# Fused gated transformer block on one core: another order of the first loads, statistics before tables, and the skip terms made by ScalarE and added a quad of heads at a time

## The reference

```python
x = x + jnp.tanh(g_xattn[0]) * _L0_xattn_ref(ctx_2048, ctx_2048, _layernorm(x, axis=-1), ssm_kernel, D, 8)
# _L0_xattn_ref: 16 heads of 8 channels, k = v = context, q = layernorm(x)
kv = jnp.einsum('bhil,bhjl->bijhl', k_, v_)            # pair products inside a head
y = irfft(rfft(kv, n=2L) * rfft(ssm_kernel, n=2L))[..., :L]   # causal convolution along l
out = y + kv * D[None, None, None, :, None]            # skip term, one number per head
out = jnp.einsum('bijhl,bhil->bjhl', out, q_)
```

## Time and profile before

| what | before |
|---|---|
| median of 3 runs | 958.02 us (956.0 to 959.27) |
| the profiled execution's own time | 956.07 us |
| its span in the trace | 953.6 us |
| PE busy | 910.1 us (95%) |
| DVE, ACT, POOL busy | 605.7, 545.4, 200.7 us |
| first block | 0 to 115.7 us of the span |

### The profile page before, as it was taken

The page is one execution under the profiler, slowest core; times in us unless marked ns, Lnnn a source line. Parts: engine busy times, 40 slices in busy tenths (PEclk is TensorE's granted clock), DMA queues, the critical chain, the costliest instruction groups (busy, mean ns, idle before and its releaser), DMA issues.

```text
span 953.6 us, 13986 instructions
## 1 busy us (share of the span) xinstructions
PE 910.1 (95%) x4744; PEld 723.5 (76%) x4744; DVE 605.7 (64%) x1396; ACT 545.4 (57%) x947; POOL 200.7 (21%) x171
## 2 busy tenths in 40 slices
PE   5799889999999999979999988999999999999998
PEld 5799758877788888846666666778788888888886
DVE  6678654555564565478888765656955466556554
ACT  3222043433444335458889675777777777777775
POOL 5899400000000001137777530000000000000000
PEclk9899999999999999999999998999999999999999
DMA  8100120323211351024554305444444344444443
GB/s 299 62 1 1 34 84 17 107 80 114 94 51 35 96 187 58 32 88 156 176 169 156 121 7 166 133 133 132 133 146 150 98 133 133 147 149 136 139 129 109
DMA packets 58101, 104.62 MB, mean 110 GB/s; under 512 B 7312, under 2 KB 13840, under 8 KB 57648
## 3 DMA queue, kind: packets, MB, share of 16 engines
q1 hardware_dynamic: 57312, 103.60, 34.0%
q10 hardware_dynamic: 720, 0.14, 0.1%
HBM read 101.29 MB, written 2.42 MB: 109 GB/s over the span
## 4 chain that ended last, share of the span: by engine, by line
PE 49%; DVE 3%; ACT 2%; issue 1%; DMA 1%; POOL 0%; DVEq 0%; SPq 0%; ACTq 0%; POOLq 0%
PE bank L1111 19%; PE bank L1078 18%; PE bank L1370 3%; PE bank L1381 2%; PE bank L1363 1%; PE bank L1362 1%; PE bank L1358 1%; PE bank L1390 1%; PE bank L534 1%; PE bank L770 1%; DVE X L668 0%; DMA Gf<-gates 0%; DVE shifted_scores L1560 0%; PE bank L752 0%; DVE max L1554 0%
## 5 line engine op out<-in xcount | busy, mean ns | idle before, releaser
L1078 PE MATMUL bank<-xhf,whif 128*128 128x512 f32 x528 | 212.0, 401 | 1.5 <-ACT rf L848 1.5
L1078 PE MATMUL bank<-xlf,whif 128*128 128x512 f32 x528 | 208.2, 394 | 0.0
L1078 PE MATMUL bank<-xhf,wlof 128*128 128x512 f32 x528 | 208.1, 394 | 0.0
L867 ACT ACTIVATE yhif<-yf 128x512 fp32r<-128x512 f32 x200 | 124.1, 622 | 86.6 <-DVE yf L952 82.5
L966 DVE TENSOR_TENSOR yf<-yf,Gf 128x512 f32<-128x512 f32 x125 | 86.5, 692 | 129.3 <-ACT yf L856 122.1
L1111 PE MATMUL bank<-yhif,whif 128*128 128x512 f32 x400 | 159.5, 399 | 7.0 <-DVE ylof L731 6.5
L1111 PE MATMUL bank<-yhif,wlof 128*128 128x512 f32 x400 | 157.9, 395 | 0.0
L1111 PE MATMUL bank<-ylof,whif 128*128 128x512 f32 x400 | 156.9, 392 | 0.0
L731 DVE TENSOR_TENSOR ylof<-yf,yhif 128x512 fp32r<-128x512 f32 x196 | 134.4, 687 | 30.0 <-ACT yhif L867 29.7
L850 ACT ACTIVATE rf<-bank 128x512 f32<-128x512 f32 x136 | 81.0, 596 | 80.7 <-PE bank L1078 80.6
L1078 PEld LDWEIGHTS bank<-xhf,whif 128*128 128x128 f32 x528 | 99.3, 188 | 24.5 <-ACT rf L848 1.9
(11 more groups left out here) (135 smaller groups left out, 1212.2 us busy)
## 6 DMA issues: line engine op xcount, KB each, us to landing
Gf<-gates SPq DMA_DIRECT2D x157, 256.0 KB, 3.7
wrawf<-in_wu SPq DMA_DIRECT2D x68, 256.0 KB, 2.6
k_blocks_sb<-in_k_blk SPq DMA_DIRECT2D x64, 256.0 KB, 4.1
wrawf<-in_wu SPq DMA_DIRECT2D x32, 384.0 KB, 3.2
v_slot<-in_v_rows SPq DMA_DIRECT2D x16, 256.0 KB, 2.7
ctx_windows<-in_ctx_win SPq DMA_DIRECT2D x3, 1024.0 KB, 11.7
toeplitz<-in_kpad SPq DMA_DIRECT2D x4, 512.0 KB, 9.2
X<-in_x SPq DMA_DIRECT2D x4, 512.0 KB, 9.3
```

Source lines behind the costliest of these rows:

```text
L867: act.activation(yhi[:, K % S, :], y[:, K % S, :], ACT.Copy).then_inc(s_yh, 1)
L1078: last = pe.matmul(o, w_[:, Nu % S, wc], x_[:, c, xs], start=(m == 0), stop=(m == 5))
```

## The change

The first load of input rows now goes ahead of the first windows and the first table. ACT issues its constants in the order D, anti-diagonal, identity instead of identity, anti-diagonal, D. ACT makes the skip blocks D[h] * anti in a new tile `skip` (16 activations of 128x128), and DVE adds them to the table with one TENSOR_TENSOR of 128x4x128 for each quad instead of four SCALAR_TENSOR_TENSOR. On DVE the statistics of part 0 stand ahead of the tables, and the tables of quads 2 and 3 stand between weighings. POOL does part 0 ahead of `pairs(1)`. PE turns group 0 after step 1 instead of step 2. The wait for the tanh gate moves from the start of group 0 to group 1.

```diff
@@ sync
+                    rows(0)
                     window_quad(0)
                     kernel_table(0)
-                    rows(0)
@@ gpsimd
                     pairs(0)
-                    pairs(1)
                     pool.wait_ge(s_mh, 1)
                     deviations(pool, "a", 0)
                     shifts(pool, "a", 0)
+                    pairs(1)
                     pairs(2)
                     pairs(3)
@@ scalar
+                    act.dma_start(dbc[:], d_skip.partition_broadcast(P)).then_inc(s_ca, 16)
+                    act.dma_start(anti[:], anti_c).then_inc(s_ca, 16)
                     act.dma_start(ident[:], ident_c).then_inc(s_c, 16)
-                    act.dma_start(anti[:], anti_c).then_inc(s_ca, 16)
-                    act.dma_start(dbc[:], d_skip.partition_broadcast(P)).then_inc(s_ca, 16)
...
+                    def skip_blocks(hq):
+                        for h in range(4 * hq, 4 * hq + 4):
+                            last = act.activation(skip[:, h, :], anti[:], ACT.Copy, scale=dbc[:, h:h + 1])
+                        last.then_inc(s_sk, 1)
+
+                    act.wait_ge(s_ca, 32)
+                    skip_blocks(0)
                     squares(0)
+                    for hq in range(1, 4):
+                        skip_blocks(hq)
+                    normed(0)
+                    squares(1)
                     act.wait_ge(s_tl, 32)
                     act.activation(tg[:], graw[:], ACT.Tanh).then_inc(s_tg, 1)
-                    squares(1)
-                    normed(0)
@@ tensor
                             convolve(g, r // 2, r % 2)
-                            if g == 0 and r == 2:
+                            if g == 0 and r == 1:
                                 for half in range(2):
                                     turn(0, half)
@@ vector
                         dve.wait_ge(s_kt[hq], 16)
-                        for h in range(4 * hq, 4 * hq + 4):
-                            last = dve.scalar_tensor_tensor(TM[:, h, 0:P], anti[:], dbc[:, h:h + 1], TM[:, h, 0:P], ALU.mult, ALU.add)
-                        last.then_inc(s_td, 1)
+                        dve.wait_ge(s_sk, hq + 1)
+                        hs = slice(4 * hq, 4 * hq + 4)
+                        dve.tensor_tensor(TM[:, hs, 0:P], TM[:, hs, 0:P], skip[:, hs, :], ALU.add).then_inc(s_td, 1)
...
-                    dve.wait_ge(s_ca, 32)
-                    table(0)
                     input_moments(0)
                     dve.wait_ge(s_st, st.n)
                     variances(dve, "a", 0)
                     negated(dve, "a", 0)
-                    for hq in range(1, 4):
+                    for hq in range(2):
                         table(hq)
-                    dve.wait_ge(s_tg, 1)
                     for g in range(NG):
                         for r in range(8):
                             weigh(g, r // 2, r % 2)
+                            if g == 0 and r in (0, 2):
+                                table(2 + r // 2)
                             if g == 0 and r < 3:
                                 input_moments(r + 1)
...
+                            if g == 1 and r == 0:
+                                dve.wait_ge(s_tg, 1)
```

More of the change, by code:

```diff
@@ L165, in build @@
             dbc = sb("dbc", [P, NH0], ctx=pa)
+            skip = sb("skip_blocks", [P, NH0, P], ctx=pa)
             s_r = deviation_sems["a"][2]
@@ L173, in build @@
             s_td = sem("a_table_ready")
+            s_sk = sem("a_skip_blocks_ready")
             s_kv = sem("a_pairs_ready")
```

## The result

The changed kernel takes 961.48 us (median of 20 runs, 955.24 to 964.96), the kernel before 958.06 in the same comparison (20 runs): a ratio of 1.0039, 95% interval 1.0025 to 1.0052. It is slower by 3.4 us, outside the range. Measured again later (e12), it was 961.53 against 958.23, ratio 1.0037 (1.0024 to 1.0049). Two executions of e7, at 1147 and 2296 us, were in a slower state and are left out of its median and ratio.

The account below looks back on a forecast made before the run. The prediction took group 1's turn, behind DVE's and POOL's nearly level chains, as the bound. A start 2 to 3.5 us earlier would shrink to 0.15 to 0.2 in the block: -0.2 from 958.02, 957.8 us, range 955.3 to 960.3.

Parts of the forecast that it names:

- What bounds it: Group 1's turn on PE at 37.16 us, behind DVE's chain ending at 32.27 and POOL's at 31.35.
- the floor of 31.35: End of POOL's large product of pairs(5), the earliest start of its power of part 1, then at 32.35.
- the landing of the identity: Identity load third on ACT's queue: lands between 4.8 and 7.4 us, where it landed first at 3.88.
- The slower rival: Late identity delays PE's warming-up and the first weighing; slower by 2.9 us from a landing at 9.8; chance 0.10.
- w: Start of DVE's first weighing: 17.4 us, up to 18.9 by the identity or 20.0 by ACT, against 20.93.
- 1.2 us of waiting on POOL: Waiting counted in DVE's chain when setting w = 18.4, beyond which each us of w costs one at the turn.
- the 12.72: DVE's chain from the first weighing to vpe's end without waits on POOL: 11.34 us plus 1.38 for two tables.
- The sum: The whole forecast change, -0.2 us; in it a table addition holds POOL up for 0.69.
- term for step 6: PE's step behind the wait takes 2.91 us at 1.2 GHz, a loss of 1.34 expected to stay the same.
- ceiling: Most the power of part 1 could gain with DVE early: 1.00 us, from 32.35 to 31.35.
- The second rival: Clearly faster: floor 1.0, clock 1.34 and group 1's load 0.6 us earlier, 954.9 or less; chance 0.11.
- The wait for POOL: Some DVE operations wait for a whole POOL multiplication under way, such as a TENSOR_SCALAR of 1.62 us.

Follow-up runs that it names:

- e12: The changed kernel measured again with no edit: 961.53 us against 958.23 for the kernel before, ratio 1.0037.
- e7: The kernel before with ACT's constants in the order D, anti-diagonal, identity and nothing else: 960.19 us against 957.88, ratio 1.0029.
- e10: e6 with POOL's power of part 1 ahead of the products of quad 5, fills of 18 and 10 matmuls: 954.94 us, ratio 0.9965.
- e6: The changed kernel with the identity first and unused matmuls, 24 ahead of the turn, 10 ahead of the last reductions: 955.38 us, ratio 0.9976.
- e11: The kernel before with only ACT's skip blocks and one TENSOR_TENSOR a quad, all orders as before: 956.94 us, ratio 0.9984.
- e3: The kernel before with 14 unused matmuls filling PE's idle time ahead of the turn: 955.57 us, ratio 0.9975.
- e8: The kernel before with unused matmuls, 14 ahead of the turn and 10 ahead of the last reductions: 954.54 us, ratio 0.9964.
- e5: The changed kernel with the identity issued first again on ACT's queue: 956.86 us against 957.88 for the kernel before, ratio 0.9993.
- e9: The changed kernel, identity third, with PE warming up on a tile DVE sets, 24 matmuls, no load needed: 957.96 us against 958.23, ratio 1.000.
- e4: The changed kernel with unused matmuls, 20 ahead of the turn and 10 ahead of the last reductions: 956.81 us, ratio 0.9984.
- e2: The changed kernel with 20 unused matmuls filling PE's idle time ahead of the turn: 958.68 us, ratio 1.0004.
- the first profile: The first profiled execution of the changed kernel, with no further edit: 958.30 us.

## Why the prediction was wrong

- *What bounds it: right.* The turn of group 1 is the point through which the first 37 us act, and two chains stand in front of it. e10 moved POOL's half and the turn came 1.43 us earlier than in e6; e11 moved DVE's half and the power started at 31.31, at the floor of 31.35.
- *The failed step: the landing of the identity,* "between 4.8 and 7.4". Its upper end came from one row, D landing third at 7.36. In the five profiles with the new loads and the identity third it landed once at 6.96 and four times at 9.2 to 9.6; third beside the old loads at 7.92. The row of before was no bound either: D in its old third place landed at 8.6 to 8.7 in the profiles of e3 and e8.
- *The slower rival was the mechanism,* with the chance of 0.10 that the bound gave it. Its threshold was a landing at 9.8 and a first weighing at 21.3 for 2.9 us. Measured in e12: 9.62, 21.37 and a turn 2.14 us late, where the rival's 1 us for each beyond w = 18.4 gives 3.0; it counted 1.2 us of waiting on POOL in DVE's chain, which took 13.04 in e12, 0.3 over the 12.72. e5 shows it by taking it away (-4.6 us), e9 by freeing PE's first work of the load (-3.5), and e4 against e8 prices the late chain alone at about 2.2. e7 (+2.3) shows that the place costs in the old kernel too, but in its profile by the clock and not by the chain.
- *The part left out: TensorE's clock.* The sum had a term for step 6, "I expect the same loss", which held for that step (2.98 against 2.91). It did not hold for the stretch: the turn ran slow too (1.12 against 0.66), and from the turn to the last reductions it is 1.25 and 0.92 longer in the two profiles, where the two of before agree within 0.1. There was no term for the last reductions: 5.08 and 6.58 us, against 3.71 in both of before. That the clock is the rest of the 3.4 us follows from the fills (1.2 us, or 1.8 by the ratios, to about 1 us); how it divides between the two places does not, as the fill at the end is within the noise. Why the same wait of 3.1 us lets the clock fall in one execution and not in the next isn't settled: e11 has the fall (5.04) with the identity first, e2 has not with it third.
- *The rest: too small to test.* Without the identity's move the change is worth -1.0 us, not to be told from none (forecast -0.2, ceiling -1.0). In the profile of e5 the turn is 0.67 earlier (forecast 0.15): POOL was held up for 0.44 by the table beside it (its two `halves` took 2.93 instead of 2.49), where the sum had 0.69. w was 17.21 in e5 (17.4). The skip blocks took 1.28 for the first four and 3.60 for the other twelve in the first profile, 0.30 to 0.32 each (0.39 taken). The second rival's own terms, 1.0 + 1.34 + 0.6, end at 955.1 and not at 954.9.
- *The wait for POOL: right.* In the first profile vpe took 1.77, the table of quad 1 2.02 where one alone takes 0.69. The Trainium skill's rule ("SBUF — State Buffer", "SBUF: two separate sides"), which the prediction weighed, excludes a DVE operation with two SBUF inputs and a POOL operation that reads SBUF for the whole instruction, and the trace agrees for the table addition beside a product. vpe, like the TENSOR_SCALAR of 1.62 that the prediction counts for the rule, has one input in SBUF, so its wait is measured but is not this case of the rule. For the power it agrees only in part: the power took 1.39 and 1.40 where a table addition was under way as it started (e12, e9), but 1.02 in the first profile, where the addition started 0.19 behind it, and that addition took 0.69, as alone.

## What to carry to other kernels

A load that the first instruction of an engine waits for belongs first in its queue, however little it seems to matter: here 64 KB moved from first to third cost 2.3 us in the old kernel and 4.6 in the new. If it can't be first, the first work can do without it: e9 got 3.5 us back with a tile that DVE sets. The landing time of one profiled execution is no bound for a load: look at several. Where TensorE idles for some microseconds ahead of short work, matmuls of no use in the gap are worth trying, and a look at whether the clock held (in e6 it did not): they gave the best time of this case, 954.54 us on the kernel before (e8), 3.3 us under it; and a gain ahead of a wait must be followed to the next wait (e10).

## What was not expected of the hardware

- The same load in the same place lands at 6.96 in one execution and at 9.62 in another of the same kernel, and the first rows at 5.86 and 7.16 with it.
- Which stretches run at 1.2 GHz differs between executions of one kernel: the turn took 0.66 us in one profile of the kernel before and 1.11 in the other, the last reductions 5.08 and 6.58 in those of the changed kernel. The slowest and the fastest of the 20 runs have mean granted clocks of 0.987 and 0.994 and lie 9.7 us apart.
